# Last stage of a decoder layer: sixteen row buffers, loads ahead of the stores, three batches combined on GpSimd

## The reference

```
x = x + self_attention(layernorm(x))          # 16 heads, local blocks of 64 and 8 global tokens
x = x + cross_attention_mlp(layernorm(x), ctx)
h = layernorm(x)
logits = einsum('btc,ec->bte', h, router_w);  top_vals, top_idx = top_k(logits, 2)
gates = sigmoid(top_vals)
moe = sum over the token's 2 experts of gate * down(silu(gate_proj) * up_proj)     # 16 experts
x = x + moe + shared_mlp(h)
```

## Time and profile before

| | us |
|---|---|
| median of 3 runs | 592.04 (591.06 to 600.29) |
| profiled execution, its own time | 596.01 |
| its span | 594.2 |
| last stage, first load issued to the end of the span | 571.65 to 594.2 |
| PE, DVE, ACT, POOL busy over the span | 501.1, 422.8, 301.7, 300.8 |
| DMA over the span, mean | 98 GB/s |

### The profile page before, as it was taken

The page is one execution under the profiler, slowest core; times in us unless marked ns, Lnnn a source line. Parts: engine busy times, 40 slices in busy tenths (PEclk is TensorE's granted clock), DMA queues, the critical chain, the costliest instruction groups (busy, mean ns, idle before and its releaser), DMA issues. The chain is left out here.

```text
span 594.2 us, 17204 instructions
## 1 busy us (share of the span) xinstructions
PE 501.1 (84%) x5995; PEld 373.6 (63%) x5995; DVE 422.8 (71%) x1256; ACT 301.7 (51%) x772; POOL 300.8 (51%) x556
## 2 busy tenths in 40 slices
PE   2969889988989989977999999999868999999700
PEld 1746666666666666645676766767644788888600
DVE  7658878888878877876898989989564334434327
ACT  2746546556555555433556565655431444444327
POOL 4744424443334433210138777777773277777730
PEclk9979989999999999996999999999988999999865
DMA  6434232344333443422523333233114344433149
GB/s 185 107 72 110 52 61 67 61 111 112 100 95 95 102 106 85 106 54 60 128 63 89 94 86 97 75 93 83 39 50 144 89 114 113 121 108 101 49 150 300
DMA packets 96004, 58.33 MB, mean 98 GB/s; under 512 B 24560, under 2 KB 92224, under 8 KB 95920
## 3 DMA queue, kind: packets, MB, share of 16 engines
q1 hardware_dynamic: 80928, 42.95, 28.3%
q0 software_dynamic: 4576, 9.91, 5.0%
q10 hardware_dynamic: 10416, 4.39, 3.1%
HBM read 20.83 MB, written 17.50 MB: 65 GB/s over the span
## 5 line engine op out<-in xcount | busy, mean ns | idle before, releaser
L735 DVE TENSOR_REDUCE nmax<-ps 128x8 f32<-128x512 f32 x128 | 85.1, 683 | 17.9 <-PE ps L1527 13.1
L632 POOL DMA_INDIRECT expert_out<-ey,xt x79 | 75.6, 958 | 42.4 <-issue 21.2
L535 POOL TENSOR_SCALAR pgq<-pgq,gstat 128x256 f32<-128x256 f32 x16 | 16.7, 1044 | 129.8 <-DVE gstat L799 129.8
L1228 ACT ACTIVATE probs<-ps 128x512 f32<-128x512 f32 x128 | 75.3, 605 | 9.5 <-PE ps L1733 5.7
L579 POOL DMA_INDIRECT expert_in<-xn,sloti x64 | 65.5, 1023 | 17.6 <-issue 17.6
L1098 DVE TENSOR_TENSOR eh<-ps,sg 128x256 f32<-128x256 f32 x40 | 17.0, 425 | 57.7 <-ACT sg L1418 57.7
L676 DVE TENSOR_SCALAR xn<-x_rows,mv,rstd 128x128 f32<-128x128 f32 x64 | 27.2, 466 | 30.1 <-POOL rstd L489 30.1
L1527 PE MATMUL ps<-kbd,qs 96*64 96x128 bf16 x512 | 38.4, 293 | 8.7 <-DMA qs<-part 7.3
L1931 PE MATMUL ps<-wgu,turned 128*128 x160 | 41.3, 380 | 0.3 <-ACT turned L1412 0.3
L1208 ACT CAST part<-res 128x512 bf16<-128x512 f32 x16 | 9.9, 618 | 61.7 <-DVE res L724 61.7
L487 POOL TENSOR_SCALAR veps<-mv 128x2 f32<-128x2 f32 x48 | 12.9, 268 | 51.1 <-DVE mv L670 39.9
(11 more groups left out here) (241 smaller groups left out, 1375.8 us busy)
## 6 DMA issues: line engine op xcount, KB each, us to landing
kbd<-part SPq DMA_DIRECT2D x192, 32.0 KB
qs<-part SPq DMA_DIRECT2D x96, 64.0 KB
xt<-expert_in SPq DMA_DIRECT2D x80, 72.0 KB
qs<-part ACTq DMA_DIRECT2D x48, 64.0 KB
ck_scr<-wgu SPq DMA_DIRECT2D x6, 512.0 KB, 2.8
ckbd<-ck_scr SPq DMA_DIRECT2D x16, 192.0 KB, 3.0
kbd<-part SPq DMA_DIRECT2D x48, 64.0 KB
wgu<-in_L_ffn_gate_up_w SPq DMA_DIRECT2D x4, 512.0 KB, 4.0
```

What stands on the lines that cost most here:

```text
L632: pool.indirect_dma_start(ys, bass.IndirectOffsetOnAxis(xt[p][:, E:E + 1].bitcast(I32), 0), ey[q % 4][:, j, :], None).then_inc(e_(f"out{q ...
L735: v.tensor_reduce(nmax[:, u, 8 * half:8 * half + 8], bank[:, :].rearrange("p (h k) -> p h k", k=64), AX.X, ALU.max, negate=True).then_inc( ...
L1228: a_.activation(probs[:, 2 * i:2 * i + 2, :], P2[i % 2][:, :].rearrange("p (j q) -> p j q", j=2), ACT.Exp, scale=SCALE).then_inc(s("probs" ...
```

## The change

Only the last stage changes, and the constant that numbers the rows.

- `row_of`: the output rows of a batch are numbered by partition first, then tile, then expert. So the four rows that partition p needs for a batch (two tiles, two experts) lie side by side, 2 KB.
- `yrow`: 16 buffers in place of eight. The first eight are where they were, the others in cvbd_all, which cross-attention used.
- `landed(b)`: each load has a semaphore of its own, with the count at which earlier stages leave it.
- SP issues all 16 loads, then the 16 stores, each after its batch is final; `summed(b)` says which semaphore tells that.
- POOLED = (5, 9, 13): POOL does these three batches by itself behind its last scatter, with four multiplications and two additions each. ALONE becomes (3, 10, 14), so ACT keeps ten batches and DVE thirteen.

```diff
-    row_of = ((t * 128 + p) * TOPK + k).reshape(128, NT * TOPK)
+    row_of = ((t // 2 * 128 + p) * 2 * TOPK + t % 2 * TOPK + k).reshape(128, NT * TOPK)
...
+        back_space = [space.bitcast(F32) for space in back_space] + [cvbd_all[:, :, :, :].rearrange("p b j c -> p (b j c)")]
+        yrow = [back_space[n][:, at:at + 2 * TOPK * E].rearrange("p (k c) -> p k c", c=E)
+                for n, size in enumerate((1024, 1024, 2048, 4096)) for at in range(0, size, 2 * TOPK * E)]
...
-        ALONE = (3, 8, 13)
+        ALONE = (3, 10, 14)
+        POOLED = (5, 9, 13)
...
+        def summed(b):
+
+            if b in POOLED:
+                return w_("set"), 8 + POOLED.index(b) + 1
+            return g_("x_out"), b + 1 - sum(a < b for a in POOLED)
...
-                sp.dma_start(yrow[b % BACK][:, :, :].rearrange("p (u k) c -> p u (k c)", k=TOPK),
-                             ys[512 * b:512 * (b + 1), :].rearrange("(u p k) c -> p u (k c)", p=128, k=TOPK)).then_inc(got, 16)
+                sp.dma_start(yrow[b][:, :, :].rearrange("p i c -> p (i c)"),
+                             ys[512 * b:512 * (b + 1), :].rearrange("(p i) c -> p (i c)", p=128)).then_inc(got, 16)
...
-            for b in range(BACK):
+            for b in range(B):
                 rows_back(b)
             for b in range(B):
-                sp.wait_ge(g_("x_out"), b + 1)
-                if b + BACK < B:
-                    rows_back(b + BACK)
+                sp.wait_ge(*summed(b))
                 sp.dma_start(ov[:, 2 * b:2 * b + 2, :], X[:, 2 * b:2 * b + 2, :]).then_inc(w_("stored"), 16)
...
+                def combine(b):
+                    xb = X[:, 2 * b:2 * b + 2, :]
+                    y = yrow[b][:, :, :].rearrange("p (u k) c -> p u k c", k=TOPK)
+                    got, base = landed(b)
+                    n = POOLED.index(b)
+                    pool.wait_ge(got, base + 16)
+                    for i in range(2 * TOPK):
+                        rows = yrow[b][:, i:i + 1, :].squeeze(1)
+                        last = g.tensor_scalar(rows, rows, gate[:, 4 * b + i:4 * b + i + 1], None, ALU.mult)
+                    last.then_inc(w_("began"), 1)
+                    pool.wait_ge(w_("began"), 2 * n + 2)
+                    g.tensor_tensor(xb, xb, y[:, :, 0, :], ALU.add).then_inc(w_("began"), 1)
+                    pool.wait_ge(w_("began"), 2 * n + 3)
+                    g.tensor_tensor(xb, xb, y[:, :, 1, :], ALU.add).then_inc(w_("set"), 1)
+
+                pool.wait_ge(r_("plan"), PLANNED + 2)
+                pool.wait_ge(h_("x"), B // 2)
+                for b in POOLED:
+                    combine(b)
...
                 for b in range(B):
-                    combine(b)
+                    if b not in POOLED:
+                        combine(b)
...
-                    if b not in ALONE:
+                    if b not in ALONE + POOLED:
                         scaled(b)
```

More of the change, by code:

```diff
@@ L27 @@
 SLOT = E + 16
-RING, BACK = 16, 8
+RING = 16
 HELD = 12
@@ L230, in decoder @@
         cqs = qs + [spare[:, PAIRS * S * i:PAIRS * S * (i + 1)].rearrange("p (j q) -> p j q", q=S) for i in range(2)]
-        ring_space = [qs[0][:, :, :].rearrange("p j q -> p (j q)"), qs[1][:, :, :].rearrange("p j q -> p (j q)"),
+        back_space = [qs[0][:, :, :].rearrange("p j q -> p (j q)"), qs[1][:, :, :].rearrange("p j q -> p (j q)"),
                       kbd[1][:, :, :, :, :].rearrange("p j a k n -> p (j a k n)")]
-        yrow = [ring_space[min(i // 2, 2)][:, 1024 * (i - 2 * min(i // 2, 2)):1024 * (i - 2 * min(i // 2, 2)) + 1024].bitcast(F32)
-                .rearrange("p (k c) -> p k c", c=E) for i in range(BACK)]
+        back_space = [space.bitcast(F32) for space in back_space] + [cvbd_all[:, :, :, :].rearrange("p b j c -> p (b j c)")]
+        yrow = [back_space[n][:, at:at + 2 * TOPK * E].rearrange("p (k c) -> p k c", c=E)
+                for n, size in enumerate((1024, 1024, 2048, 4096)) for at in range(0, size, 2 * TOPK * E)]
         CV_BANKS = (6, 4, 5, 7)
@@ L337, in decoder, with landed @@
         GOT = {True: 16 * 3 * NP, False: 16 * NP}
+        def landed(b):
+            own = [(g_(f"got{q}"), 0) for q in range(4)] + [(e_(f"in{q}"), 16 * (TILES // 4)) for q in range(4)]
+            own += [(w_("x_first"), 32), (w_("x_next"), 16), (w_("x_more"), 16), (w_("experts"), 16 * 5)]
+            own += [(s_("got"), GOT[True] * B), (c_("got"), GOT[False] * B), (e_("zeros"), 16 * 2 * NE), (w_("ck_put"), 16 * (NP + B))]
+            return own[b]
+        def summed(b):
+            if b in POOLED:
+                return w_("set"), 8 + POOLED.index(b) + 1
+            return g_("x_out"), b + 1 - sum(a < b for a in POOLED)
         block = ctx.enter_context(nc.Block())
@@ L462, in rows_back @@
             def rows_back(b):
-                got, base = (g_(f"got{b % 4}"), 0) if b % BACK < 4 else (e_(f"in{b % 4}"), 16 * (TILES // 4))
-                sp.dma_start(yrow[b % BACK][:, :, :].rearrange("p (u k) c -> p u (k c)", k=TOPK),
-                             ys[512 * b:512 * (b + 1), :].rearrange("(u p k) c -> p u (k c)", p=128, k=TOPK)).then_inc(got, 16)
+                got, _ = landed(b)
+                sp.dma_start(yrow[b][:, :, :].rearrange("p i c -> p (i c)"),
+                             ys[512 * b:512 * (b + 1), :].rearrange("(p i) c -> p (i c)", p=128)).then_inc(got, 16)
             for q in range(4):
                 sp.wait_ge(e_(f"out{q}"), 16 * (TILES // 4 - q // 3))
-            for b in range(BACK):
+            for b in range(B):
                 rows_back(b)
             for b in range(B):
-                sp.wait_ge(g_("x_out"), b + 1)
-                if b + BACK < B:
-                    rows_back(b + BACK)
+                sp.wait_ge(*summed(b))
                 sp.dma_start(ov[:, 2 * b:2 * b + 2, :], X[:, 2 * b:2 * b + 2, :]).then_inc(w_("stored"), 16)
@@ L1115, in combine @@
                     xb = X[:, 2 * b:2 * b + 2, :]
-                    y = yrow[b % BACK][:, :, :].rearrange("p (u k) c -> p u k c", k=TOPK)
+                    y = yrow[b][:, :, :].rearrange("p (u k) c -> p u k c", k=TOPK)
+                    before = b - sum(a < b for a in POOLED)
                     if b in ALONE:
-                        got, base = (g_(f"got{b % 4}"), 0) if b % BACK < 4 else (e_(f"in{b % 4}"), 16 * (TILES // 4))
-                        dve.wait_ge(got, base + 16 * (b // BACK + 1))
+                        got, base = landed(b)
+                        dve.wait_ge(got, base + 16)
                         for k in range(TOPK):
                             if k:
-                                dve.wait_ge(g_("first"), b + 2 + ALONE.index(b))
+                                dve.wait_ge(g_("first"), before + 2 + ALONE.index(b))
                             for u in range(2):
@@ L1129, in combine @@
                         return
-                    dve.wait_ge(g_("scaled"), 2 * TOPK * (b + 1 - sum(a < b for a in ALONE)))
+                    dve.wait_ge(g_("scaled"), 2 * TOPK * (before + 1 - sum(a < b for a in ALONE)))
                     v.tensor_tensor(xb, xb, y[:, :, 0, :], ALU.add).then_inc(g_("first"), 1)
-                    dve.wait_ge(g_("first"), b + 1 + sum(a < b for a in ALONE))
+                    dve.wait_ge(g_("first"), before + 1 + sum(a < b for a in ALONE))
                     v.tensor_tensor(xb, xb, y[:, :, 1, :], ALU.add).then_inc(g_("x_out"), 1)
@@ L1434, in scaled @@
                 def scaled(b):
-                    got, base = (g_(f"got{b % 4}"), 0) if b % BACK < 4 else (e_(f"in{b % 4}"), 16 * (TILES // 4))
-                    act.wait_ge(got, base + 16 * (b // BACK + 1))
+                    got, base = landed(b)
+                    act.wait_ge(got, base + 16)
                     for i in range(2 * TOPK):
-                        y = yrow[b % BACK][:, i:i + 1, :].squeeze(1)
+                        y = yrow[b][:, i:i + 1, :].squeeze(1)
                         a_.activation(y, y, ACT.Copy, scale=gate[:, 4 * b + i:4 * b + i + 1]).then_inc(g_("scaled"), 1)
```

## The result

The changed kernel is slower: its median is 599.57 us, that of the kernel before 592.7. The two medians lie 6.9 us apart. The ratio to the kernel before, over the executions in the chip's faster state alone, is 1.0096 (95% interval 1.0072 to 1.0121), which is 5.7 us (4.3 to 7.2). The forecast was 594.0 with a range of 589.5 to 598.0. The direction was right and the size was not. Within 2% was given 0.96, and within 2% it is.

A forecast was written before the change was run, and what follows sets the result against it. The last stage was taken to be bound by DVE and GpSimd excluding each other: 7.0 plus 8.7, 15.7 us from 578.2, with DVE ending at 593.9, 2.0 later than before; 592.0 + 2.0 = 594.0, range 589.5 to 598.0.

The forecast's parts named there:

- The store behind it takes the same 2.3 us: End of the last stage: the span ends 2.3 us after DVE's last add, for the last store's issue and landing.
- The part on GpSimd: Last stage: three batches on GpSimd (POOL) take 11.5 us; starting at 578.2, batch 13 is ready at 589.8 if undisturbed.
- the forecast's 2.0: Last stage: DVE ends with batch 15 at 593.9, 2.0 us after the 591.9 of before.
- the second rival: Last stage: DVE and GpSimd hardly disturb each other; batch 13 and two stores behind it set the end, median 591.0; chance 0.22.
- the sign that the prediction named for it: Last stage: DVE adds at 0.425 throughout, and SP's last wait on w_set (GpSimd) instead of x_out.
- the sum: Last stage from 578.2: excluding parts of DVE, 7.0, and GpSimd, 8.7, run serially, 15.7 us, ending at 593.9 or after.
- How DVE and POOL exclude each other: Last stage: one waits until the other has read; 0.285 of a DVE add, 0.20 fused, 0.435 POOL scaling, 0.585 POOL add.
- POOL's prices: Last stage: a POOL scaling costs 0.576 us and an add 0.727, so a batch takes 3.76.
- ACT: Last stage: 13 gated batches become 10, 3.6 us less; ACT ends at about 586.6 in place of 590.7.
- Loads first: Last stage, SP's queue: 16 loads at 0.38 to 0.50 each put the first store at 577.7 to 579.7 instead of 577.14.
- The stores behind POOL: Last stage: SP stores in order, so stores 13, 14 and 15 wait for batch 13; last store at 590.9.
- 2 KB pieces: Last stage's loads: nothing gained, 0.75 us per 256 KB at 349 GB/s, or fewer gaps; batch 5 at 578.2, or 579.8.

The follow-up runs named there:

- early_drain: The changed kernel with one more POOL drain right behind its last scatter; ratio to the kernel before 1.0041 (1.0009 to 1.0073).
- pairs: Small kernel without the layer: DVE's and POOL's last-stage operations alone, then side by side; 16 DVE adds took 5.5 us alone, 5.9 beside scalings, 10.7 beside adds.
- loads_first: The changed kernel with no batch on POOL and DVE alone on batches 3, 8 and 13; ratio to the kernel before 0.9963 (0.9932 to 0.9995).
- alone_0: The changed kernel with nothing on POOL and DVE alone on batches 0, 4, 8 and 12; ratio to the kernel before 0.9971 (0.9938 to 1.0005).

## Why the prediction was wrong

**The step that failed is one that it doesn't have: POOL's closing drain, a term put at nothing.** "The store behind it takes the same 2.3 us" took the end of the program for the end of the last store. The part on GpSimd asked what the three batches cost there and whom they hold up, and not what POOL's program does after them. The trace of before had the row, a POOL DRAIN of 13.7 us, in instructions that aren't counted as busy and so stand in no window or timeline. In the changed kernel the program ended 7.4 us behind POOL's last add, not behind the last store. The drain is worth 4.1 us of the stage (early_drain), and without it the end lies 2.0 us above before by the profile and 2.6 by the ratio.

**Those 2.0 are not the forecast's 2.0; that they agree is luck.** The forecast had DVE last, with its final add 22.2 us behind the first load (593.9 less 571.65); it came at 19.0. It had POOL through near 19.4; it was 21.2. The path is that of the second rival, POOL's batch 13 with two stores behind it in SP's queue, and the sign that the prediction named for it came: SP's last wait for a batch was for POOL. The rival's condition held too, a loss of DVE under 60% of the 5.4 us of the sum; it was 2.3, 43%. The rival had 1.0 faster, and the path came out 2.0 slower, because POOL began 0.9 later behind the first load than it had and took 2.2 longer.

- *How DVE and POOL exclude each other.* The mechanism was right and the sizes were not. A scaling was to keep DVE out for 0.435; pairs shows next to nothing (0.5 us for 16 adds), while it is held back itself (0.60 to 0.83). POOL's add was taken at 0.585, and measured 0.5. With 12 scalings and 6 adds DVE lost 2.3 us in the changed kernel (its 32 operations sum to 14.9 us and would to 12.6 undisturbed), not the 5.4 that the sum gave it. Its 14 adds from 577.9 on have a mean of 0.53, where 0.6 was said, and nearly all of what they lose they lose beside POOL's adds, as here:

```profile
580.07 0.83 DVE L1167 TENSOR_TENSOR x_rows<-x_rows,kbd 128x256 f32<-128x256 f32 x1
580.69 0.79 POOL L663 TENSOR_TENSOR x_rows<-x_rows,kbd 128x256 f32<-128x256 f32 x1
580.82 0.94 DVE L1165 TENSOR_TENSOR x_rows<-x_rows,cvbd_all 128x256 f32<-128x256 f32 x1
```

  The inference came from single meetings, two of three with POOL as the one that waits; they say that it waits, and not what DVE loses. The Trainium skill ("SBUF — State Buffer", "Who interferes with whom") has the order of issue decide which of the two blocks. For POOL's scalings beside DVE's adds the trace of pairs doesn't agree: nearly all of the loss is POOL's (2.8 us, and 0.5 on DVE).
- *POOL's prices.* The scaling at 0.576 measured 0.602 alone (pairs), the add at 0.727 measured 0.722. POOL's three batches took 13.7 us in place of 11.5. At the durations of pairs alone their 18 operations would sum to 11.6, and they sum to 13.4: 1.9 of the difference comes with DVE beside them, 0.3 from the dearer scaling. Batch 5's first scaling began 7.5 us behind the first load; 6.5 was taken, with 8.1 as the far end.
- *ACT.* Predicted to end 14.95 behind the first load, it ended at 15.3, without a wait after its first row. Right.
- *Loads first.* First store predicted 6.0 to 8.0 behind the first load, it went at 8.0 (577.17). Right, at the late end: a load's issue took 0.43, not 0.33.
- *The stores behind POOL* were said for the case without contention and hold in the one with it: three waits, 6.7 us.
- *2 KB pieces* were bounded by nothing and fewer gaps. 390 GB/s against 346 to 349 is what they bring to the loads, and since DVE bounds the stage the end sees little of it.

**Why three batches off DVE bring it so little.** A batch that POOL takes saves DVE two adds, 0.79 us. What it costs DVE is 2 x 0.5 by pairs and 2.3 / 3, or 0.8, in the changed kernel. On DVE POOL's help comes to next to nothing: the last add comes at 19.0 with three batches fewer and at 19.5 with none fewer (loads_first).

## What to carry to other kernels

Before work is put on an engine at the end of a program, look at what its queue still has to do behind that work: in this trace the closing DRAIN of a POOL that had scattered ran 7.2 us past its last instruction, and it is hidden only while other engines work that long after it. If POOL must work late, a drain put where it waits anyway takes the cost there once. Where two engines share work on the same memory, price what each operation of the one takes from the other, not only its own duration; here POOL's two-input adds took from DVE what they spared it.

## What the runs showed of the hardware that was not expected

- POOL's drain takes 7.2 us in this kernel (nine executions), counted from POOL's last instruction or, where POOL reaches the drain only later, from there (alone_0), whether the last scatter ended 0, 3.4 or more than 20 us before; with an earlier drain in between it is 0.07. In small kernels it is 0.07 us with no scatter of its own, 0.16 with one, 2.7 with 32 and 2.5 with 143. What sets the size between 2.5 and 7.2 is open.
- Of DVE's two-input adds and POOL's scalings by a column, side by side, it is POOL's that are held back: DVE 417 to 442 ns, POOL 602 to 833. With DVE's fused operations beside the scalings it is rather DVE's: 347 to 396, POOL 602 to 646. Adds on both sides: DVE 417 to 742, POOL 722 to 905.
- The wait for the others at the program's end appears as a wait of SP for PE's queue, though PE had ended 30 us before.
